# Query and key projections earlier on TensorE, ScalarE's roundings in another order

## The reference

```python
q = apply_rope((x @ wq.T).reshape(B, S, 16, 128).transpose(0, 2, 1, 3))
k = apply_rope((x @ wk.T).reshape(B, S, 4, 128).transpose(0, 2, 1, 3))
v = (x @ wv.T).reshape(B, S, 4, 128).transpose(0, 2, 1, 3)
k, v = jnp.repeat(k, 4, axis=1), jnp.repeat(v, 4, axis=1)
k = k * key_weights[None, :, None, None]
scores = jnp.einsum('bhqd,bhkd->bhqk', q, k) * 128 ** -0.5
attn = jax.nn.softmax(jnp.where(causal, -jnp.inf, scores), axis=-1)
out = jnp.einsum('bhqk,bhkd->bhqd', attn, v)
return out.transpose(0, 2, 1, 3).reshape(B, S, 2048) @ wo.T
```

## Time and profile before

| | before |
|---|---|
| time, median of 3 runs | 863.23 us (861.54 to 864.09) |
| the profiled execution | 861.93 us, its span 860.1 us |
| TensorE busy | 789.0 us, 92% of the span |
| VectorE busy | 674.2 us, 78% |
| GpSimd busy | 515.9 us, 60% |
| ScalarE busy | 501.9 us, 58% |
| chain that ended last | PE 59%, POOL 17%, DVE 10%, issue 7%, ACT 6% |

### The profile page before, as it was taken

One profiled execution on the slowest core, in us unless ns is written; L12 is line 12 of the kernel. 1 busy time (PEld: TensorE's weight loads), 2 busy tenths in 40 slices (PEclk: granted clock), 3 DMA queues, 4 the chain that ended last, 5 costly groups with the idle time before them and its releaser, 6 DMA issues.

```text
span 860.1 us, 15634 instructions
## 1 busy us (share of the span) xinstructions
PE 789.0 (92%) x4520; PEld 684.6 (80%) x4520; DVE 674.2 (78%) x1888; ACT 501.9 (58%) x1250; POOL 515.9 (60%) x408
## 2 busy tenths in 40 slices
PE   7899999578899899999989989999998998899996
PEld 4688877467788888888878888888887888788885
DVE  6889895796877867778687786777868777989876
ACT  3565555548566575665756657566575664544543
POOL 4745569665776867768577686776857760203212
PEclk9999999789999999999999999999999999999999
DMA  9235502111123121212311313121131110000001
GB/s 298 97 101 184 197 13 63 26 24 38 26 74 79 31 49 28 82 45 65 85 24 37 94 28 85 26 72 45 28 98 24 37 26 1 1 1 26 1 26 49
DMA packets 30629, 50.11 MB, mean 58 GB/s; under 512 B 3970, under 2 KB 12802, under 8 KB 30594
## 3 DMA queue, kind: packets, MB, share of 16 engines
q1 hardware_dynamic: 30596, 49.71, 20.6%
HBM read 18.76 MB, written 9.96 MB: 33 GB/s over the span
## 4 chain that ended last, share of the span: by engine, by line
PE 59%; POOL 17%; DVE 10%; issue 7%; ACT 6%; DMA 1%; POOLq 0%; ACTq 0%; DVEq 0%; SPq 0%
PE pt L1771 6%; PE pj L1690 4%; PE pj L1691 4%; PE pj L1692 4%; POOL gc L1305 4%; POOL at_rot L1307 4%; POOL at_rot L1303 4%; POOL at_ql L1295 3%; PE sc L1756 3%; DVE at_pr L1427 3%; PE sc L1758 3%; PE sc L985 3%; PE sc L987 3%; PE sc L986 3%; PE sc L1757 3%
## 5 line engine op out<-in xcount | busy, mean ns | idle before, releaser
L1295 POOL TENSOR_TENSOR at_ql<-at_rot,at_qh 128x512 fp32r<-128x512 f32 x64 | 82.5, 1288 | 113.0 <-ACT at_qh L1542 112.9
L1427 DVE TENSOR_SCALAR at_pr<-at_pr,at_inv 128x512 f32<-128x512 f32 (+7 forms) x256 | 143.9, 623 | 2.3
L1590 ACT ACTIVATE at_pth<-pt 128x512 fp32r<-128x512 f32 x192 | 91.1, 528 | 83.2 <-PE pt L1771 82.9
L1583 ACT ACTIVATE at_pr<-at_pr,at_low 128x512 f32<-128x512 f32 (+7 forms) x256 | 134.0, 530 | 8.9 <-DVE at_low L1417 7.8
L1771 PE MATMUL pt<-ident,at_pr 128*128 128x128 f32 x640 | 93.2, 287 | 34.9 <-DVE at_pr L1427 24.1
L1433 DVE TENSOR_TENSOR at_ptl<-pt,at_pth 128x512 fp32r<-128x512 f32 x192 | 105.9, 593 | 2.9 <-ACT at_pth L1590 2.9
L1771 PEld LDWEIGHTS pt<-ident,at_pr 128*128 128x128 f32 x640 | 76.0, 147 | 39.6 <-issue 33.8
L1303 POOL TENSOR_TENSOR at_rot<-ga,cos 128x512 f32<-128x512 f32 x80 | 105.4, 1318 | 2.3 <-POOL at_ql L1295 2.3
L1307 POOL TENSOR_TENSOR at_rot<-at_rot,gc 128x512 f32<-128x512 f32 x80 | 103.0, 1287 | 6.3
L1305 POOL TENSOR_TENSOR gc<-gc,sin 128x512 f32<-128x512 f32 x80 | 105.7, 1321 | 1.6 <-DMA gc<-ga 1.6
L1417 DVE CUSTOM_DVE_ANT_0 at_pr<-sc,at_mask 128x512 f32<-128x512 f32 (+2 forms) x192 | 91.4, 519 | 12.5 <-PE sc L1758 12.5
(11 more groups left out here) (279 smaller groups left out, 2222.2 us busy)
## 6 DMA issues: line engine op xcount, KB each, us to landing
gc<-ga SPq DMA_DIRECT2D x160, 128.0 KB, 2.3
ga<-in_attn_w SPq DMA_DIRECT2D x8, 384.0 KB, 5.0
at_wo<-attn_split SPq DMA_DIRECT2D x6, 512.0 KB, 4.2
attn_split<-gb SPq DMA_DIRECT2D x6, 384.0 KB, 2.4
attn_split<-gc SPq DMA_DIRECT2D x6, 384.0 KB, 3.3
gb<-attn_split SPq DMA_DIRECT2D x6, 384.0 KB, 3.7
x<-in_x SPq DMA_DIRECT2D x4, 512.0 KB, 9.0
e_raw<-in_expert_w SPq DMA_DIRECT2D x8, 256.0 KB, 6.0
```

The lines of the kernel that those rows point to most:

```text
L1295: pool.tensor_tensor(to, rotated(r), lead.bitcast(F32), ALU.subtract).then_inc(ql_done, 1)
L1427: dve.tensor_scalar(a, a, inv[kind][:, k:k + 1], None, ALU.mult).then_inc(nm_done, 1)
L1583: act.activation(a, a, ACT.Exp, bias=low[kind][:, k:k + 1], scale=-1.0, accum_out=tot[kind][:, k:k + 1]).then_inc(ex_done, 1)
L1590: act.activation(pth[kind][:, cols], pt[k % 2][:, 0:FLEN[kind][k]], ACT.Copy).then_inc(hi_done, 1)
```

## The change

Nothing is computed otherwise; instructions move on two engines, in steps 0 to 14 (in step 15 one move of ScalarE alone).

```diff
 # scalar, step
-                    if more1:
+                    if u == 2 and ahead and not first:
+                        raw_out(s + 1, 4)
+                    if u % 2 == 0 and more1:
                         prob_lead(s1, u1, 0)
                         prob_lead(s1, u1, 1)
                     if more2:
                         exps(s2, u2, range(2))
-                    if u == 0 and ahead:
-                        rotated_lead(act, s + 1, 0)
+                    if u != 1 and ahead:
+                        rotated_lead(act, s + 1, (0, None, 3, 4)[u])
                     if more2:
                         exps(s2, u2, range(2, BT))
+                    if u == 1 and ahead and not first:
+                        raw_out(s + 1, 3)
+                    if u == UNITS - 1 and ahead == 2:
+                        raw_out(s + 2, 0)
                     if first and u < 2:
                         raw_out(s + 1, u + 3)
-                    elif not first and u in (1, 2) and ahead:
-                        raw_out(s + 1, u + 2)
-                    if u == (1 if first else 2) and ahead:
+                    if u == 1 and first:
+                        value_out(s + 1)
+                    if u % 2 and more1:
+                        prob_lead(s1, u1, 0)
+                        prob_lead(s1, u1, 1)
+                    if u == 2 and ahead and not first:
                         value_out(s + 1)
                     if first and u in (1, 2):
                         norm_rows(*NORMS[u - 1])
+                    if ahead and u < 2:
+                        rotated_lead(act, s + 1, u + 1)
                     if u == UNITS - 1 and ahead == 2:
-                        raw_out(s + 2, 0)
                         raw_out(s + 2, 1)
-                    if ahead:
-                        rotated_lead(act, s + 1, u + 1)
 # tensor, step
+                    if u == 2 and ahead and not first:
+                        query(s + 1, 3)
                     if more2:
                         scores(s2, u2, range(3) if u2 % 2 == 0 else range(BT))
+                    if u == 1 and ahead and not first:
+                        query(s + 1, 2)
+                    if first and u == 1:
+                        query(s + 1, 3)
+                        value(s + 1)
+                    if u == UNITS - 1 and ahead == 2:
+                        key(s + 2)
                     if more1:
                         transpose_p(s1, u1, (0, 1))
...
-                    if first and u == 1:
-                        query(s + 1, 3)
-                        value(s + 1)
                     if u == 1 and not first:
-                        if ahead:
-                            query(s + 1, 2)
                         output_early(s - 1, not ahead)
                     if u == 2 and ahead and not first:
-                        query(s + 1, 3)
                         value(s + 1)
                     if u == UNITS - 1 and ahead == 2:
-                        key(s + 2)
                         query(s + 2, 0)
```

## The result

| | before | after |
|---|---|---|
| time, median (runs) | 863.6 us (4) | 923.24 us (4), 922.36 to 925.21 |
| ratio after to before, 95% interval | | 1.0683 to 1.0717 |
| span of the profiled execution | 860.1 us | 920.7 us |
| TensorE, VectorE, GpSimd busy | 789.0, 674.2, 515.9 us | 823.1, 743.1, 521.1 us |
| VectorE, L1427 (`normalise`) | 143.9 us | 217.7 us |

A forecast was written before the change was run, and what follows sets the result against it. TensorE all but bounds the 35.7 us step. Later `normalise` cost 4.0 us a step, less 0.7 in pass 0; 14 × 3.35 = 47 us on 861.93 gave 909 us, own range 885 to 922, 8 in 10 858 to 926.

The forecast's parts named there:

- the two holes: TensorE's waits of 1.71 us in pass 1 and 0.85 us in pass 2, to be filled, saving 2.56 us a step.
- The meeting of unit 3: Pass 1: `normalise` misses GpSimd's quiet stretch, takes 4.3 us in place of 1.93 and ends 4.2 us late.
- The meeting in pass 2: Unit 0's `normalise` meets GpSimd because of the earlier `rotated_lead`; blocking adds 3.1 us to VectorE, from 1.48 us.
- GpSimd's pause there: Pass 2: the move takes 3.95 us of idleness from GpSimd, ahead of the third query's `rest`.
- The next step's start: From unit 0's `mask_min` at 482.9 to its `normalise`'s end at 491.5, then 8.8 us to unit 2's `mask_min`.
- the way from the start of `mask_min` to the first exponential: Pass 0: 0.7 us won by TensorE running ahead; pass 2: exponentials start 0.7 us behind `mask_min`.
- TensorE's idle time: Whole step: TensorE idle 6 us of 39.0, new holes opening before the fourth score chunk and unit 0's transposes.
- The ends: Step 0, where `normalise` meets GpSimd already, and step 15, where GpSimd is done, were put at nothing.
- The filled holes: Rival: TensorE's order is the bound; both holes gone 826 us, only the third query's 842; chance 0.17.
- The rival of no change: Unit 3's `normalise` escapes GpSimd at 1.2 us; step 35.6 to 35.9 us, 862 to 866 us; chance 0.12.
- The worse rival: Pass 3's `normalise` also meets GpSimd, TensorE's clock falls; 1.5 to 2.6 us a step more, 930 to 945; chance 0.09.

The follow-up runs named there:

- e7: The kernel before with TensorE's part of the change, but the next key's projection back behind the transposes; 844.0 us.
- e4: The changed kernel with `prob_lead` back ahead of the exponentials in passes 1 and 3; 894.6 us.
- e5: The changed kernel with `normalise` written as a `tensor_scalar` that also sums its result into a spare column; 853.7 us.
- e9: The changed kernel with both `prob_lead` and the two `rotated_lead` back in their old places, only the earlier `raw_out` left; 855.2 us.
- e6: The kernel before with `normalise` written as the `tensor_scalar` that also sums its result; 868.7 us.

## Why the prediction was right, and where it was off

**What bounds a step.** Right: TensorE all but did, and the two holes were filled, but what was won there was small beside what the rest lost. With the two queries moved alone (e7) the first hole shrank to 0.34 us and the second, which hangs on GpSimd's chain, stayed at 0.84; that gave the 20 us that the prediction had for the third query alone.

**The meeting of unit 3.** This was the step on which the sign hung: `normalise` at 476.5, GpSimd at 476.55. Measured, it started 0.12 us ahead of GpSimd and took 4.06 us against the 4.3 summed. The margin was not as thin as 0.05 us looks: to escape, `normalise` had to start 0.6 us sooner, when GpSimd's pause began, and starting inside GpSimd's work would have cost nearly as much (3.58 us). e4 undid the meeting and the delay ahead of it (29 us less).

**The meeting in pass 2.** Right in kind and size: 4.55 us where 4.55 was forecast. GpSimd's pause there did not vanish, as I had said it would. It was 4.07 us, but ahead of 437.41 and not beside `normalise`.

**The next step's start.** `mask_min` of unit 0 to its `normalise`'s end: 434.10 to 443.27, 9.2 us, forecast 8.6. From there to the next `mask_min` of unit 2: 443.27 to 451.91, 8.6 us, forecast 8.8.

**The term that was mis-sized** is the way from the start of `mask_min` to the first exponential, in two passes. In pass 0 I took 0.7 us off, on the ground that TensorE would run ahead. The first exponential stood 1.25 us behind (412.44 to 413.69), where it had been 1.47: 0.2 us won, not 0.7. TensorE was not ahead: its transposes of unit 0 had waited 1.56 us for `normalise` in pass 3, at 443.41, and from there to those of the next pass 0, at 451.72, it had no pause above 0.15 us. In pass 2 I let the first exponential follow 0.7 us behind, and it took 1.25 (434.10 to 435.35), because it stands behind a `prob_lead`, whose transposes had waited the 2.02 us above:

```profile
434.59 0.87 ACT L1590 ACTIVATE at_pth<-pt 128x512 fp32r<-128x512 f32 x2 [4.22 <-PE pt L1779]
435.35 0.72 ACT L1583 ACTIVATE at_pr<-at_pr,at_low 128x512 f32<-128x512 f32 x1
```

That is 0.5 us twice; the shorter `normalise` of unit 3 and smaller pieces gave half of it back, so the step is 39.5 us and not 39.0. From unit 2's `normalise` in step 1 to the one in step 15, which is 14 steps, the kernel before took 500.8 us and the changed one 553.3: 52.5 us more where 47 had been summed.

**TensorE's idle time** was forecast at 6 us a step. It was 4.5 in the step read, and 3.1 and 3.4 in the two beside it. TensorE's busy time grew with the same matmuls, from 33.1 us to 34.9 in the step read, and to 36.4 in the other two, where the granted clock was 0.96 and not 1.00. What made it grow at a clock of 1.00 is open. These steps took 39.5 to 39.8 us all the same.

**The ends** were put at nothing and cost 8.1 us. `normalise` of step 1, unit 2, began at 214.91 us before and at 219.19 after, so 4.3 us were lost in step 0 already. There too the `rotated_lead` of pass 2 moved in between exponentials, and the `normalise` of that pass took 4.48 us where it had taken 1.47. From unit 2's `normalise` of step 15 on, the rest of the program took 144.4 us before and 148.2 after; TensorE was busy 2.8 us longer in that stretch, at a granted clock of 0.97 against 0.99.

**A wrong name for a wait.** I expected TensorE to wait for L1417 ahead of the fourth chunk. It stood one place earlier, at the transposes, and waited for `prob_rest` (L1433) to free their bank; both hang on the same late VectorE, but `prob_lead` comes behind these transposes, and that made the 1.25 us of pass 2.

**The rivals.** The filled holes did not win because two meetings were added, not because the holes were worthless: e5, with the meetings gone and every instruction in its new place, is 1.2% faster than before. The rival of no change would have needed `prob_lead` 0.6 to 0.7 us sooner, and e4 shows that even then the loss of pass 2 stays (894.6 us); that rival's 35.6 to 35.9 us a step was too low by about 2. The worse rival did not come about: pass 3's `normalise` ran free, and where the granted clock was lower the step was no longer than 39.8 us.

## What to carry to other kernels

Before moving work into a hole, list the instructions whose duration depends on what another engine does at that moment, here `tensor_scalar` on SBUF against any GpSimd work, and check where the move puts each against that engine's pauses. Here `normalise` came 0.6 us too late for a pause and took 4.06 us where it had taken 1.93. Then ask what waits for the instruction: the longer `normalise` of e7 and e9 cost nothing that shows. When a change has several parts, time each alone: the two queries' projections were worth 20 us, and every other part of the change cost time or brought nothing. A further move, rounding the key earlier, was found by asking what the remaining wait hung on. A form of the instruction that is slower alone but never blocked is worth a trial where orders are to be changed freely; in a finely placed order (e6) it only cost.

## What the runs showed of the hardware that was not expected

The form of `tensor_scalar` that also sums its result (TENSOR_SCALAR_CACHE_REDUCE in the trace) took 0.75, 0.68, 0.61 and 0.54 us for 512 to 320 columns and 0.48 to 0.28 us for 256 to 64, with a 0.08 us read of the sum, beside a working GpSimd. The plain one took 1.48 us for all four wide ones alone and 4.6 beside GpSimd. The Trainium skill, "SBUF — State Buffer", section "Who interferes with whom", excludes this form from those that contend; e5's rows agree. GpSimd pays too, but little: some of its instructions beside a plain `normalise` took 1.39 to 1.48 us instead of 1.28.
